# Second pair pass of a four-layer graph network: the score transfers issued by GpSimd instead of SyncE

## What is computed

```
D[i,j,:] = |h[i,:] - h[j,:]|
p        = D @ W1.T + b1                     # 64 numbers for each pair (i,j)
p        = batchnorm(p over all graphs and pairs) * g1 + be1
s[i,j]   = leaky_relu(p, 0.01) @ W2 + b2     # one score for each pair
att      = softmax(where(A > 0, s, -9e15))
y        = (att @ h) @ Wg.T + bg
out      = concat(h, leaky_relu(batchnorm(y))) @ Wt.T + bt
```

## Time and profile before

| | |
|---|---|
| median of 3 runs | 2103.72 us (2099.93 to 2104.76) |
| time of the profiled execution | 2111.06 us |
| its span, first to last instruction | 2109.2 us |
| mean granted TensorE clock | 0.940 |
| busy: PE, DVE, ACT, POOL | 83%, 82%, 66%, 28% of the span |
| transfers in q1 (SyncE) | 106360 packets, 283.37 MB |
| transfers in q0 (GpSimd) | 256 packets, 0.56 MB |
| bytes moved over the span | 139 GB/s |

### The profile page before, as it was taken

One profiled execution on the slowest core, in us unless ns is written; L12 is line 12 of the kernel. 1 busy time (PEld: TensorE's weight loads), 2 busy tenths in 40 slices (PEclk: granted clock), 3 DMA queues, 4 the chain that ended last, 5 costly groups with the idle time before them and its releaser, 6 DMA issues. The chain is left out here.

```text
span 2109.2 us, 43810 instructions
## 1 busy us (share of the span) xinstructions
PE 1749.2 (83%) x13754; PEld 1106.5 (52%) x13771; DVE 1721.6 (82%) x2689; ACT 1396.4 (66%) x3229; POOL 593.0 (28%) x449
## 2 busy tenths in 40 slices
PE   2967677777776899996899999999999588888886
PEld 1855566566563666665465555555555144444445
DVE  5978888888885777875899999999998577777777
ACT  0533333333334989995588888888888577777774
POOL 1530000000002545443354444544444111111110
PEclk9978988988887999999999999999999899999999
DMA  6000000000000000000255555555555899999993
GB/s 180 1 13 1 1 0 0 0 0 0 0 1 4 7 6 6 4 7 21 81 220 225 223 219 224 219 224 220 226 221 219 324 340 344 344 339 341 338 330 87
DMA packets 123567, 292.98 MB, mean 139 GB/s; under 512 B 21376, under 2 KB 57608, under 8 KB 123288
## 3 DMA queue, kind: packets, MB, share of 16 engines
q1 hardware_dynamic: 106360, 283.37, 36.1%
q10 hardware_dynamic: 16896, 8.39, 1.4%
q0 software_dynamic: 256, 0.56, 0.1%
HBM read 150.45 MB, written 141.82 MB: 139 GB/s over the span
## 5 line engine op out<-in xcount | busy, mean ns | idle before, releaser
L1316 POOL TENSOR_TENSOR pair_ring<-hd 128x2048 f32 (+1 forms) x64 | 269.5, 4212 | 310.7 <-DVE pair_ring L1341 310.7
L1401 ACT ACTIVATE v_hid<-v_psW 128x1024 f32<-128x1024 f32 x256 | 263.4, 1029 | 85.2 <-PE v_psW L1439 85.2
L771 DVE TENSOR_REDUCE m_part<-m_psS 128x128 f32<-128x2048 f32 (+1 forms) x128 | 258.9, 2022 | 74.6 <-PE m_psS L638 74.6
L1337 DVE TENSOR_TENSOR pair_ring<-v_psX,hd 128x2048 f32<-128x2048 f32 x128 | 292.2, 2286 | 17.7 <-PE v_psW L1439 17.6
L1439 PE MATMUL v_psW<-pair_ring,p_w1T 128*64 128x512 f32 x1024 | 288.9, 597 | 0.0
L1404 ACT ACTIVATE v_junk<-v_psW 128x1024 bf16<-128x1024 f32 x256 | 263.3, 1029 | 0.0
L638 PE MATMUL m_psS<-m_onehot,m_tableT 32*128 32x128 f32 x3584 | 156.4, 314 | 125.4 <-DVE m_part L771 119.0
L1439 PE MATMUL v_psW<-pair_ring,l_w1T 128*64 128x512 f32 (+1 forms) x1024 | 252.5, 587 | 0.0
L1430 PE MATMUL v_psW<-p_ends,v_weights 128*64 128x512 bf16 x1536 | 235.2, 381 | 3.2 <-DMA v_fold<-in_c_fold_dram 3.2
L1587 DVE SCALAR_TENSOR_TENSOR pair_ring<-pair_ring 128x1024 f32<-128x1024 f32 x128 | 156.4, 1225 | 65.9 <-ACT pair_ring L1654 65.9
L638 PEld LDWEIGHTS m_psS<-m_onehot,m_tableT 32*128 32x128 f32 x3584 | 132.5, 213 | 145.2 <-issue 76.9
(11 more groups left out here) (260 smaller groups left out, 3360.5 us busy)
## 6 DMA issues: line engine op xcount, KB each, us to landing
pair_hidden<-v_hid SPq DMA_DIRECT2D x256, 512.0 KB, 2.6
pair_ring<-pair_hidden SPq DMA_DIRECT2D x128, 1024.0 KB, 7.4
adj_ring<-in_adj_dram ACTq DMA_DIRECT2D x16, 256.0 KB, 5.7
x_all<-in_x_dram ACTq DMA_DIRECT2D x16, 256.0 KB, 5.8
out_dram<-x_all SPq DMA_DIRECT2D x16, 256.0 KB, 2.3
pair_scores<-s_rot SPq DMA_DIRECT2D x64, 32.0 KB, 5.1
s_fwd<-pair_scores SPq DMA_DIRECT2D x64, 32.0 KB, 5.1
s_wide<-pair_scores SPq DMA_DIRECT2D x64, 32.0 KB, 5.5
```

What stands on the lines that cost most here:

```text
L771: nc.vector.tensor_reduce(part[:, i % 2, r, :], psS[:, :, 0:w].rearrange("z q (c i) -> z i q c", i=N), AX.XY, ALU.max).then_inc(reduced, 1)
L1316: nc.gpsimd.tensor_tensor(D[:, home(u, SLABS - 1), :].rearrange("c (h d i) -> c h d i", h=2, i=N), one, far, ALU.subtract).then_inc(psub_d ...
L1337: nc.vector.tensor_tensor(slab(s), own, windows(hd, n, s)[1], ALU.max).then_inc(max_done, 1)
L1401: nc.scalar.activation(hid[:, s, :], psW[:, buf, :], ACT.Identity, accum_out=hsum[:, bass.ds(m, 1)]).then_inc(evacuated, 1)
```

## The change

The scatter and the two gathers of each graph are moved from SyncE to GpSimd. SyncE keeps only the loads, in the same order and behind the same semaphores. GpSimd does, in step n, the gathers of graph n-3, the scatter of graph n-2 and then its own part for graph n-4, which until now it did alone. GpSimd's loop over the steps, with registers for the addresses, becomes straight code. GpSimd waits at the start of the pass until the scratch matrices are filled, as before, so the wait of SyncE for it is gone.

```diff
@@ block.sync
-                def scatter(m):
-                    sp.wait_ge(rot_ready, done(m))
-                    dst = scratch[m % 4]
-                    sp.dma_start(bass.AP(dst.tensor, dst.offset + 1, [[2 * N + 1, N], [1, HID]]), rot[:, m % 2, :]).then_inc(written[m % 2], 16)
-
-                def gather(m):
-                    sp.wait_ge(written[m % 2], 16 * (m // 2 + 1))
-                    sp.wait_ge(m_mm, done(m - 2))
-                    src = scratch[m % 4].rearrange("(i j) -> i j", j=2 * N)
-                    sp.dma_start(fwd[0:HID, m % 2, :], src[0:HID, 0:N]).then_inc(back[m % 2], 16)
-                    sp.wait_ge(fwd_ready, done(m - 2))
-                    sp.dma_start(wide[HID:N, m % 2, :], src[HID:N, HID:HID + N]).then_inc(back[m % 2], 16)
-
-                for n in range(B + 3):
-                    if n >= 3:
-                        gather(n - 3)
-                    if n == 2:
-                        sp.wait_ge(prefilled, 64)
-                    if 2 <= n < B + 2:
-                        scatter(n - 2)
-                    if n + 2 < B:
-                        sp.wait_ge(p0_mm, done(n))
-                        load(2 * n + 4)
-                        sp.wait_ge(affine_done, done(2 * n + 1))
-                        load(2 * n + 5)
+                for n in range(B - 2):
+                    sp.wait_ge(p0_mm, done(n))
+                    load(2 * n + 4)
+                    sp.wait_ge(affine_done, done(2 * n + 1))
+                    load(2 * n + 5)
@@ block.gpsimd
-                def step(n, p, t, zero, one, two, three, four, five, six, seven):
-                    if four:
-                        m = n - 4
-                        pool.wait_ge(xo_mm, done(m - 2))
-                        nc.gpsimd.tensor_copy(hx[:, p, :], hd[:, bass.ds(m * DUP, N)]).then_inc(hx_ready, 1)
-                        xs = k.x[:, bass.ds(m * C, C)]
-                        nc.gpsimd.tensor_tensor(xs, xs, k.bt[:, :], ALU.add).then_inc(xb_ready, 1)
-                graphs(pool, step)
+                def scatter(m):
+                    pool.wait_ge(rot_ready, done(m))
+                    dst = scratch[m % 4]
+                    pool.dma_start(bass.AP(dst.tensor, dst.offset + 1, [[2 * N + 1, N], [1, HID]]), rot[:, m % 2, :]).then_inc(written[m % 2], 16)
+
+                def gather(m):
+                    pool.wait_ge(written[m % 2], 16 * (m // 2 + 1))
+                    pool.wait_ge(m_mm, done(m - 2))
+                    src = scratch[m % 4].rearrange("(i j) -> i j", j=2 * N)
+                    pool.dma_start(fwd[0:HID, m % 2, :], src[0:HID, 0:N]).then_inc(back[m % 2], 16)
+                    pool.wait_ge(fwd_ready, done(m - 2))
+                    pool.dma_start(wide[HID:N, m % 2, :], src[HID:N, HID:HID + N]).then_inc(back[m % 2], 16)
+
+                def part_of_x(m):
+                    pool.wait_ge(xo_mm, done(m - 2))
+                    nc.gpsimd.tensor_copy(hx[:, m % 2, :], hd[:, bass.ds(m * DUP, N)]).then_inc(hx_ready, 1)
+                    xs = k.x[:, bass.ds(m * C, C)]
+                    nc.gpsimd.tensor_tensor(xs, xs, k.bt[:, :], ALU.add).then_inc(xb_ready, 1)
+
+                for n in range(2, B + 4):
+                    if 3 <= n < B + 3:
+                        gather(n - 3)
+                    if n < B + 2:
+                        scatter(n - 2)
+                    if n >= 4:
+                        part_of_x(n - 4)
```

## The result

The changed kernel takes 2125.39 us (median of 14 runs, 2116.13 to 2140.59); the kernel before, in as many runs beside it, 2109.0 us (2099.93 to 2120.87). The ratio is 1.0083, 95% interval [1.0062, 1.0104]: slower by 13 to 22 us. The forecast was 2105.7 us and no measurable difference, the range ended at 2123. A change can be told from none at about 0.2%, so the sign is certain, and it is the one to which 0.36 was given.

A forecast was written before the change was run, and what follows sets the result against it. A closed ring through TensorE and ScalarE, 6.42 us a turn, was taken as the bound. Terms -1 + 0 + 1.5 + 0 + 0 + 1.5 = +2.0 us on the profiled 2109.2 us, carried to the runs' median: 2105.7 us, range 2100 to 2123.

The forecast's parts named there:

- the one to which 0.36 was given: Whole kernel: slower by over 0.2%, chance 0.22 + 0.14 = 0.36; no measurable difference had 0.52, faster 0.12.
- Loads on SyncE alone: SyncE's queue: three issues fewer gain 0 in regular turns, -1 us at the pass's start (bounds 0 and -9.5).
- Same bytes in another queue: Data queues: small transfers now run between the second load's packets and delay it; +1.5 us (bounds -0.5 and +7.8).
- GpSimd issues three transfers: GpSimd: 1.63 us of issues a turn delay `hx`, which has 4 us of cover before TensorE needs it; price 0.
- The ring of scatter and gather: GpSimd: scatter landing, 5.3 us, plus two issues, 1.09 us, closes at 6.39 us inside the 6.42 us turn; price 0.
- the ring binds: Rival, chance 0.22: landing of 5.7 us makes GpSimd's ring 6.79 us; +15.9 us after cover, about 2122 us.
- The Trainium skill's rule: First byte about 0.6 us for SyncE's transfers, about 1 us for GpSimd's; ring 6.59 us, some +5 us.
- End of the pass: After the last loads: three landings on the path, each 0.5 us longer from GpSimd; +1.5 us (bounds -0.6 and +10.5).

The follow-up runs named there:

- e1: The changed kernel itself, run again with no edit for a second profile; ratio 1.0080 to the kernel before, median 2128.83 us.
- e7: The changed kernel, with GpSimd issuing 27 extra transfers of 512 bytes ahead of the pass's first scatter; ratio 1.0159 to the kernel before, 2145.99 us.
- e3: The changed kernel, with GpSimd's step reordered: scatter first, then `hx` and the bias addition, then the gathers; ratio 1.0004 to the kernel before, 2108.38 us.
- e6: The kernel before, with only the scatter moved to GpSimd; SyncE keeps the gathers, ahead of its loads; ratio 0.9985, 2106.22 us.
- e2: The changed kernel, with GpSimd making `hx` and the bias addition ahead of its gathers and scatter; ratio 1.0041 to the kernel before, 2124.00 us.
- e9: The changed kernel, with 96 one-element GpSimd memsets behind the filling transfers at the start of the pass; a single execution, 2153.57 us.
- e12: The changed kernel, with GpSimd issuing the scatter between the two gathers, `hx` still behind all three; ratio 1.0021 to the kernel before, 2117.39 us.
- e5: The kernel before, with only the two gathers moved to GpSimd; SyncE keeps the scatter, ahead of its loads; ratio 1.0054, 2122.36 us.
- e10: Scatter and gathers of even graphs issued by GpSimd, those of odd graphs by SyncE as in the kernel before; ratio 0.9994 to it, 2106.99 us.
- e11: The kernel with only the scatter on GpSimd, run again with more rounds; ratio 0.9983 to the kernel before, 2108.16 us.
- e8: The kernel before, all transfers still on SyncE, with the scatter ahead of the gathers in each step; ratio 0.9999, 2109.82 us.

## Why the prediction was wrong

**Loads on SyncE alone (-1).** SyncE's wait took the place of the issues, as said. It grew to 5.7 us a turn and not to some 4: SyncE's gathers had also waited for the mask product, 83.4 us in 53 turns, which the text left out. At the start the gain did not come: 0 to 9 took 1.2 us longer in the profile after and 0.3 in e1, beside scatter of the same size among the other runs (51.7 to 54.9, e7 aside). No run shows the -1.

**Same bytes in another queue (+1.5).** About right in size. L1653 waited 2.1 us for loads in 7 turns, 0.5 in 2 before. Turns of 6.45 to 7 us lost 2.5 us in the profile after and 1.1 before: +1.4. In e1 it was 4.8 us, so +3.7. It depends on when the small transfers go, not on the queue: e3 and e6 have no such turn.

**GpSimd issues three transfers (0).** The issues took 0.53, 0.52 and 0.56 us, as costed (1.61 for 1.63). `hx` had 4 us of cover in a good turn, as said: copied from 1800.95, read by L1732 from 1805.08. But the text took that cover as a constant. It is measured from the gathers ahead of `hx`, and the gathers move when the ring is late. It was gone in the second turn after the stall (0.61 us of waiting at 1961.64), and e2 shows that this queueing is about half of the loss.

**The ring of scatter and gather (0).** This is the step that failed: it asked only whether one landing of 5.1 or 5.3 us plus two issues of 1.09 us fits in the turn, and priced the ring at nothing because it did. The ordinary landings were not to blame: 4.9 us in the median of the 34 turns ahead of the stall, under the 5.33 at which the text let the ring bind. Three things were missing. First, a lag: on GpSimd the gather starts 0.28 to 0.29 us behind the landing (on SyncE, read the same way, 0.02 to 0.06), so that the ring binds from 5.04 us on and not from 5.33. Second, a ring with 0.2 us of room can't make a large delay good. The text gave it 4.1 us of cover to use up slowly; one stall of 2.9 us used up most of that at once. Third, the landing itself grew once the ring was late: 4.6 to 6.6 us, median 5.7, in the eleven turns after the stall, all of which waited for it, and 5.8 in e9's late turns. That makes a ring of 7.2 to 7.3 us, and in it TensorE and VectorE wait.

Why the landing grows is not shown. Most of the late scatters start within 3 us behind the next turn's loads, but those of e3 and e6 start 1.5 us after the second load as well and land in 5.0; what they don't have is two gathers just ahead of them. Nor is it shown that SyncE's ring would have stood such a delay. In its queue the next loads stay behind a late scatter, but no run held one up. The late state ended after the turn of 10.12 us, and in e9 after those of 10.53 and 9.92; it did not end after the one of 9.86, nor in e1 after any of its three long turns.

The rival "the ring binds" had the right place and a size of +20 us for 54 turns at 0.37 each; the change lost 13 to 22 us, but in few turns at up to 3.7 each, and with the clock's part in them. That its total of +15.9 us comes near the measured difference of the medians, 16.4, is luck. The range missed the median by 2.4 us. The measured kernel before was also 5.3 us above the 2103.72 of the three runs that the forecast was laid on.

**The Trainium skill's rule** (DMA: Bandwidth & Descriptors, Latency and other measured facts), a later first byte for GpSimd's transfers, is not seen in the landings: with no loads beside them 1.8 to 1.9 us from GpSimd against 1.7 to 1.9 from SyncE. Under load, 5.0 us in e6 against 5.1, the two can't be told apart by it, since SyncE's stand behind the loads in their queue. What was longer on GpSimd lies ahead of the issue, the 0.29 us. The estimate by the rule was 6.59 us for the ring; ahead of the stall it was 6.2.

**End of the pass (+1.5).** +1.7 in the profile after, +4.1 in e1, where TensorE waited 5.6 us for `hx` there. The +1.7 is a hit by luck: the last scatters landed in 1.8 to 1.9 us, no later than before, and VectorE's wait of 0.62 us for the last gather was gone instead of longer.

**Open.** The stall of 2.8 to 2.9 us came in each of the seven profiles in which GpSimd issues over 128 of the pass's 32 KB transfers (after, e1, e2, e3, e7, e9, e12), always at the 129th of them, whichever line that was (`wide`, `fwd` or the scatter), and in none that issues 128 or fewer (e5, e6, e10, e11). 27 small transfers more or 96 instructions more did not move it. When it came, 5184 packets had gone through q0 in e7 and 4320 in the profile after, e3 and e12, but 4.74 and 4.73 MB. So it goes with the bytes or with the number of transfers of this size, and not with the number of packets; no run here shows what it is. It was also not tried to take it away alone, and how much of the loss would be left without it is open. e9 shows that some can be: its 23 late turns lie before the stall.

## What to carry to other kernels

A closed ring of waits (here: a scatter, its landing, the gather behind it, the next scatter behind that) must not only fit in the turn but have room, since with its room a delay is made good. Count in it the lag from landing to issue, and price it in the phase that it would have when late, not in the one that it has now. If there is little room, cut the ring by order before thinking of engines: with the scatter ahead of the gather the same move cost nothing that can be measured. It gained nothing either: no order tried beat the kernel before. And a cover measured in a good turn holds for what stands in front of the instruction in the queue; whatever is late there uses it up first.

## What the runs showed of the hardware that was not expected

- A GpSimd queue stopped once for 2.8 to 2.9 us at the 129th 32 KB transfer that it issued, in seven profiles.
- From a landing that came last to the gather's start GpSimd needed 0.28 to 0.29 us, SyncE 0.02 to 0.06.
- The landing of a 32 KB transfer differs with where in the turn it starts: from GpSimd's queue medians of 4.8 and 5.8 us in one execution. In SyncE's queue it came 8.4 to 8.6 us after the second load's issue, whether it started 3.4 us after it (5.1 us to landing) or 1.2 to 1.3 us after it (7.3 us; e8, e5).
- A wait of TensorE of 2.7 or 2.9 us was followed by the lower clock (0.90 and 0.83 over 10 us), and the turn lost up to 3.7 us. In e10 and e12 it also followed a wait of 1.5 and 1.8 us, where a load had come 0.3 and 0.6 us late, and the turn lost 2.0 us.
